# A two-layer transformer block on one core: first-layer gate as tanh straight from PSUM, second-layer low parts subtracted by GpSimd

## What is computed

```python
# layer 0, feed-forward: fp4_linear quantises both operands, then multiplies
gate = fp4_linear(x, w_gate)
y = fp4_linear(x, w_up)
h = jax.nn.silu(gate) * y
return fp4_linear(h, w_down)
# quantisation: scale = max(max|block| / 6, 1e-12); values go to the grid times scale

# layer 1, attention
q = (x @ Wq.T + bq).reshape(b, n, G, hpg, HD)
k = (x @ Wk.T + bk).reshape(b, n, G, HD)
scores = jnp.einsum('bqghd,bkgd->bghqk', q, k) * scale
attn = jax.nn.softmax(scores, axis=-1)
```

## Time and profile before

| | |
|---|---|
| runs | 1472.44 us median (1469.91 to 1474.29) |
| the profiled execution | 1470.66 us, its span 1468.9 us |
| TensorE busy | 1311.4 us (89%), 6337 matmuls |
| VectorE busy | 1088.7 us (74%), 2289 instructions |
| ScalarE busy | 845.8 us (58%), 1621 instructions |
| GpSimd busy | 110.8 us (8%), 227 instructions |
| chain that ended last | PE 71%, DVE 15%, ACT 7% |

### The profile page before, as it was taken

How to read it: one execution, slowest core, us unless ns; L and a number is a source line. 1 busy time by engine, 2 the same in 40 slices (tenths; PEclk the granted TensorE clock), 3 DMA queues, 4 the chain that set the end, 5 groups by cost and what they waited for, 6 DMA issues and landing times.

```text
span 1468.9 us, 19049 instructions
## 1 busy us (share of the span) xinstructions
PE 1311.4 (89%) x6337; PEld 563.3 (38%) x6337; DVE 1088.7 (74%) x2289; ACT 845.8 (58%) x1621; POOL 110.8 (8%) x227
## 2 busy tenths in 40 slices
PE   4688889889999965899999999999999999999884
PEld 3354445344443432433333333333433333333322
DVE  3677696688645668778888788888879888987324
ACT  2445535554555421177777666777666776777660
POOL 2010010001010100000000002000110000000033
PEclk9669899899999975689999999999999999999897
DMA  3000000000000000000000000000000000000000
GB/s 100 1 1 1 1 1 1 0 1 1 1 1 1 0 1 0 1 1 1 2 1 1 1 1 9 1 1 1 1 1 8 1 1 2 1 1 1 1 8 8
DMA packets 9010, 6.13 MB, mean 4 GB/s; under 512 B 2184, under 2 KB 8272, under 8 KB 8912
## 3 DMA queue, kind: packets, MB, share of 16 engines
q1 hardware_dynamic: 8912, 4.91, 1.2%
HBM read 3.66 MB, written 1.05 MB: 3 GB/s over the span
## 4 chain that ended last, share of the span: by engine, by line
PE 71%; DVE 15%; ACT 7%; issue 4%; POOL 1%; DMA 1%; SPq 1%; DVEq 0%; POOLq 0%; ACTq 0%
PE ps L749 24%; PE ps L730 16%; PE ps L650 8%; DVE MP L1161 7%; PE ps L726 6%; ACT PR L926 4%; PE ps L655 4%; PE ps L646 2%; PE ps L712 2%; ACT QO L825 1%; PE ps L661 1%; PE ps L679 1%; DVE ps L1158 1%; PE ps L615 1%; PE ps L690 1%
## 5 line engine op out<-in xcount | busy, mean ns | idle before, releaser
L926 ACT ACTIVATE PR<-ps 128x512 f32<-128x512 f32 (+2 forms) x1344 | 699.1, 585 | 414.1 <-PE ps L730 224.3
L1161 DVE TENSOR_REDUCE MP<-ps 128x1 f32<-128x512 f32 x1216 | 764.2, 682 | 133.9 <-PE ps L650 87.4
L749 PE MATMUL ps<-PR,V 128*32 128x512 f32 (+2 forms) x2688 | 435.6, 605 | 0.7 <-ACT OS L825 0.7
L730 PE MATMUL ps<-Q,KO 64*128 64x512 f32 x1024 | 363.1, 466 | 26.6 <-ACT PR L926 20.6
L650 PE MATMUL ps<-KO,Q 64*128 64x512 f32 x1024 | 354.5, 447 | 16.3 <-DVE MP L1161 12.2
L730 PEld LDWEIGHTS ps<-Q,KO 64*128 64x128 f32 x1024 | 153.6, 186 | 350.3 <-ACT PR L926 290.3
L650 PEld LDWEIGHTS ps<-KO,Q 64*128 64x128 f32 x1024 | 164.4, 191 | 85.0 <-DVE MP L1161 47.9
L726 PE MATMUL ps<-QO,KO 97*128 97x512 f32 (+3 forms) x320 | 144.7, 464 | 21.2 <-ACT PR L926 18.8
L655 PE MATMUL ps<-KO,QO 96*128 96x512 f32 (+2 forms) x320 | 127.9, 441 | 19.5 <-DVE QO L1137 13.7
L749 PEld LDWEIGHTS ps<-PR,V 128*32 128x32 f32 (+1 forms) x2688 | 74.1, 116 | 130.6 <-issue 60.4
L726 PEld LDWEIGHTS ps<-QO,KO 97*128 97x128 f32 x320 | 62.8, 201 | 152.0 <-ACT PR L926 97.0
(11 more groups left out here) (179 smaller groups left out, 748.7 us busy)
## 6 DMA issues: line engine op xcount, KB each, us to landing
Q<-MR SPq DMA_DIRECT2D x64, 2.0 KB
result<-V SPq DMA_DIRECT2D x4, 256.0 KB, 2.3
H<-in_L_attn_wq SPq DMA_DIRECT2D x1, 512.0 KB, 6.7
HQT<-in_L_attn_wo SPq DMA_DIRECT2D x1, 512.0 KB, 5.0
ew<-in_L_ffn_expert_w SPq DMA_DIRECT2D x1, 512.0 KB
bq<-in_L_attn_bq SPq DMA_DIRECT2D x12, 0.1 KB
wd<-in_L_ffn_w_down SPq DMA_DIRECT2D x1, 176.0 KB, 3.7
wg<-in_L_ffn_w_gate SPq DMA_DIRECT2D x1, 128.0 KB, 4.4
```

What stands on the lines that cost most here:

```text
L730: m = nc.tensor.matmul(dst[:, :], KO1[rows, g, kt * P:(kt + 1) * P], Q1[rows, it, h // 2, :], start=True, stop=True)
L749: nc.tensor.matmul(dst, VO[layer][:, kt, g, :], PR[:, u % NP_RING, q0:QC], start=kt == 0, stop=kt == key_tiles(layer, c) - 1).then_inc(pv_ ...
L926: nc.scalar.activation(PR[:, u % NP_RING, q0:QC], ps[:, 8 - nb + u % nb, q0:QC], ACT.Exp, scale=SCALE[layer]).then_inc(exp_done, 1)
L1161: v.tensor_reduce(MP[:, buf, h, q, kc:kc + 1], bank[:, 0:w], AX, ALU.max).then_inc(free, 1)
```

## The change

- **Gate.** ScalarE now writes `tanh(gate / 2)` from the PSUM bank to `H` for each of the four `gate` items. VectorE then computes `(H + 1) * bank`, which is twice SiLU, and frees the bank (L1185 of the new kernel). The step `silu` and its table loads are gone from the list. The factor two is taken out by a 0.5 where `down` is added to the residual (the instruction has three operands now, in `y0` with a factor of 1), and the quantiser's floor is 2e-12 for `H`.
- **Low parts.** For each `q1` and `k1` ScalarE first writes `bank + bias` as fp32 to one of two SBUF tiles (`WHOLE`), then the low part as before, and frees the bank. GpSimd waits for that and subtracts (L1047), and a new semaphore `tailed` tells PE (before its maxima) and ScalarE (before it reuses a tile, two items later). VectorE's `tails` are gone.
- **Buffers.** One of the two `WHOLE` tiles is the memory of the first-layer gate and up weights; the key-down and latent-up weights now load into memory of `H` and `HQT`.

```diff
-                    + gaps("2 3 1 1 1 1 2 1 1 1", [("xq", c)] + [("gate", q) for q in range(QT)] + [("silu",)]
+                    + gaps("2 3 1 1 1 2 1 1 1", [("xq", c)] + [("gate", q) for q in range(QT)]
                            + [("up", q) for q in range(QT)]))
...
+        WHOLE = (sb("WHOLE", [P, QC])[:, :], flat(wgu[:, 0:QC // D, :]))
...
-        IN_PARTS = ("q0", "k0", "k1", "q1")
+        IN_PARTS = ("q0", "k0")
+        BY_POOL = ("q1", "k1")
...
   (PE, before a max)
-                        if name in at:
+                        if name in tails_at:
+
+                            pe.wait_ge(tailed, tails_at[name])
...
   (ScalarE)
+                if kind == "gate":
+
+                    full()
+                    nc.scalar.activation(H[:, item[1], :], bank[:, 0:FF], ACT.Tanh, scale=0.5).then_inc(gated, 1)
...
+                if kind in BY_POOL:
+
+                    t = tails_at[0]
+                    if t >= len(WHOLE):
+                        act.wait_ge(tailed, t + 1 - len(WHOLE))
+                    dst, bias, low_bias, low = of_parts(item)
+                    nc.scalar.activation(WHOLE[t % len(WHOLE)], bank, ACT.Identity, bias=bias)
+                    i = nc.scalar.activation(dst, bank, ACT.Identity, bias=low_bias, scale=low)
+                    tails_at[0] += 1
...
-                    elif kind == "silu":
-
-                        j = gate_at[0]
-                        act.wait_ge(side_free[j % NS], n.side // NS + j // NS + 2)
-                        nc.scalar.activation(H[:, :, :], H[:, :, :], ACT.Silu).then_inc(act_out, 1)
...
   (GpSimd)
+                    if kind in BY_POOL:
+
+                        pool.wait_ge(side_free[k % NS], n.side // NS + k // NS + 2)
+                        dst = of_parts(step)[0]
+                        nc.gpsimd.tensor_tensor(dst, WHOLE[tails % len(WHOLE)], dst.bitcast(f32),
+                                                ALU.subtract).then_inc(tailed, 1)
+                        tails += 1
...
   (VectorE)
-            def tails(dst, bank, bias):
-
-                return v.scalar_tensor_tensor(dst, bank, bias, dst.bitcast(f32), ALU.add, ALU.subtract)
...
+                elif kind == "gate":
+                    h = H[:, item[1], :]
+                    dve.wait_ge(gated, n.gates + cnt.gates)
+                    v.scalar_tensor_tensor(h, h, 1.0, bank[:, 0:FF], ALU.add, ALU.mult).then_inc(free, 1)
...
                 elif kind in ("y0", "down"):
-                    link(v.tensor_tensor(R[:, :, :], tiles, chunk_of(item[1]), ALU.add))
+                    part = 1.0 if kind == "y0" else 0.5
+                    link(v.scalar_tensor_tensor(R[:, :, :], tiles, part, chunk_of(item[1]), ALU.mult, ALU.add))
```

More of the change, by code:

```diff
@@ L475, in __init__ @@
                 self.heads = sum(k in IN_PARTS for k in kinds)
+                self.tails = sum(k in BY_POOL for k in kinds)
                 self.rstd = sum(k in ("y0", "down", "y1", "stats") for k in kinds)
                 self.acts = sum(k in BY_SCALAR for k in kinds)
+                self.gates = kinds.count("gate")
                 self.logits = kinds.count("logits")
@@ L899, in side_item @@
                     i = copy(XQT[:, :], bank)
-                elif kind == "gate":
-                    i = copy(H[:, item[1], :], bank[:, 0:FF])
                 elif kind == "hqT":
@@ L1042, in link, with quantise @@
                 dve.wait_ge(chain, S["links"])
-            def quantise(stage, out, src, rows, width, end):
+            def quantise(stage, out, src, rows, width, end, least=1e-12):
                 nb = width // FB
```

67 lines of the change are left out of this document (34 added, 33 removed).

## The result

The changed kernel took 1477.14 us (median of 20 runs, 1471.33 to 1482.12) where the kernel before took 1473.35 (20 runs, 1469.52 to 1478.85). The ratio is 1.0029, with a 95% interval of 1.0015 to 1.0043: slower by some 4 us. Forecast were 1465.3 us, a range of 1451 to 1477, and a chance of 0.57 for faster. The mean of the four is 1.0019, so "0.1 to 0.3% slower" is what holds. Two executions in the whole record, of 1735 and 1893 us at a mean clock of 0.64 and 0.55, are left out of all ratios.

A forecast was written before the change was run, and what follows sets the result against it. PE was taken as the bound, with VectorE on the chain only beside layer 1's experts and ScalarE's exponentials throughout. Terms -7.0 + 3.2 - 5.0 + 1.5 + 0.1 = -7.2 gave 1463.5 us, or 1465.3 at the median; range 1451 to 1477.

The forecast's parts named there:

- Gate: Layer 0, chunks 0 to 3: removing SiLU and its table loads gains 7.0 us, range -2.1 to -14.
- 2.6 was forecast: Layer 0, chunk 2: gain from PE's 2.00 us idle at the SiLU and two slower passes behind it, 2.6 us.
- 1.3 was forecast: Layer 0, chunk 0: gain from PE's idle 0.97 and 0.32 us at the SiLU, taken as 1.3 us.
- first product with `up` 1.15 us behind the last tanh: Layer 0, chunk 3: tanh, wake-up and three-operand instruction take 1.15 us instead of 3.3, so 2.1 us gained.
- Keys: Low parts of 16 keys, layer 0 and its end: moving them to ScalarE and GpSimd costs 3.2 us, -2 to +6.
- 1.7 was forecast: Layer 0, chunk 2: last clip waits behind GpSimd's subtractions, so PE's last products come 1.7 us late.
- Queries: Layer 1, low parts of q1: VectorE's relief beside the experts gains 5.0 us, ScalarE's second activation costs 1.5.
- Rival A: Layer 1: each of 28 second activations costs its 0.60 us, 16.8 instead of 1.5; slower, 1480.5 us; chance 0.15.
- GpSimd's subtraction of 1.27 us delays nobody: Layer 1: some 27 maxima of other queries stand between a q1 and its first reader, so the subtraction costs nothing.
- Rival D: GpSimd's subtractions block VectorE instructions with two SBUF operands; five stops cost 6.4 us, 1471.7 us in all; chance 0.05.
- ScalarE's term: Layer 1: 0.60 us more per q1, 28 of 32 counted; five places at 0.3 give +1.5 us, range 0 to 17.
- rival C: Layer 0 gives nothing back: only chunk 3's 2.1 us remain, late clips cost twice 3.2; 1473.4 us; chance 0.16.

The follow-up runs named there:

- The mean of the four: Four timings of the changed kernel's instructions against the kernel before: 1.0029 and 1.0027 under its own name, 1.0014 and 1.0006 in two kernels with the same instructions.
- the empty step: Kernel before with the new gate, an empty step left in the list where the SiLU was: 1.0006 and 1.0004; the changed kernel with it: 1.0012.
- the one without their subtraction: New gate and moved buffers, VectorE's three-operand instruction of the 32 q1 left out and nothing in its place: 0.9929 of the kernel before.
- the kernel with the wait: Changed kernel, GpSimd's subtractions that follow an output chunk's normalisation in the list waiting until it is done: 0.9987 of the kernel before.
- another chain: New gate with moved buffers 0.9987; changed kernel with the queries' low parts back on VectorE 0.9978; changed kernel, mean of two timings, 1.0028.
- three pairs: Without and with GpSimd's wait for normalisations: keys back on VectorE 1.0008, 0.9987; changed kernel 1.0027, 0.9987; new gate plus unread subtractions 1.0020, 0.9951.
- the kernel with the extra subtraction: New gate with moved buffers, VectorE's tails kept, plus one unread GpSimd subtraction per q1: 1.0020 of the kernel before.

## Why the prediction was wrong

*Gate: forecast -7.0, measured -4.1* (0.9972, with -2 to -6.5 by single runs, and none with the empty step). The loads went, and PE's idle time behind the SiLU with them. The steps differ by chunk. Only chunk 2's can be read at a nearly level clock (0.98 before, 1.00 after): its stretch is 3.67 us shorter with the gate alone (71.10 against 74.77) and 2.52 in the changed kernel, which pays the 1.14 us for the two q1 there; 2.6 was forecast. Chunk 1's is 1.56 us shorter in the changed kernel's first profile and 1.4 longer in its second, so its 1.0 is neither borne out nor refuted. Chunk 0 gave nothing, where 1.3 was forecast: its stretch is 0.67 longer in the changed kernel and 0.6 to 2.3 in those of the gate alone. PE's idle time at the place shrank to 0.27 us, behind VectorE's product:

```profile
165.91 0.83 PE L695 MATMUL ps<-WUT,XQT 128*128 128x352 f32 x2 [0.27 <-DVE H L1188]
```

Why the stretch does not get shorter for it I have not settled. In chunk 3 the forecast had the first product with `up` 1.15 us behind the last tanh, as the earlier trace rows:

```profile
555.90 0.46 ACT L877 ACTIVATE H<-ps 128x352 f32<-128x352 f32 x1 [0.23 <-PE ps L695]
...
556.49 0.52 DVE L1185 SCALAR_TENSOR_TENSOR H<-H,ps 128x352 f32<-128x352 f32 x1 [0.17 <-ACT H L877]
557.05 0.69 DVE L1181 TENSOR_REDUCE MP<-ps 128x1 f32<-128x512 f32 x1
557.77 1.07 DVE L1188 TENSOR_TENSOR H<-H,ps 128x352 f32<-128x352 f32 x2
```

It is 1.87, for a maximum stands between them in VectorE's queue: 1.4 gained, not 2.1. What came of it hung on the clock: two profiles of the same gate-alone kernel have 154.01 us at 0.72 and 150.14 at 0.74 for the stretch that before took 152.61 at 0.73. A term of 2 us can't be read from one profile where PE switches between its two clock levels.

*Keys: forecast +3.2, measured -1.3 to +2.9 by the timings and +1.8 by the one stretch that can be read.* The step at the last clips of chunk 2 was right to a tenth: 1.7 was forecast. The other 1.5, for chunks 0, 1 and 3, lies where the clock moves, and no run shows it. ScalarE's last activation, GpSimd and PE, as the earlier trace rows:

```profile
520.26 0.77 ACT L888 ACTIVATE KO<-ps,bk_low,const 128x512 fp32r<-128x512 f32 x1
...
521.11 1.30 POOL L1047 TENSOR_TENSOR KO<-wgu,KO 128x512 fp32r<-128x512 f32 x1 [0.24 <-ACT KO L888]
522.37 0.29 POOL L1018 TENSOR_SCALAR_AFFINE_SELECT PR<-PR 128x128 f32<-128x128 f32 x1
...
522.71 0.43 PE L765 MATMUL ps<-PR,V 128*64 128x128 f32 x2 [0.58 <-POOL PR L1018]
```

1.81 us longer in every profile with the keys' subtraction on GpSimd, 0.0 in every one without.

*Queries: forecast -5.0 + 1.5, measured +3 to +7 by the timings.* The relief of VectorE was sized right (5.1 by the stretches). Rival A, at 16.8, is refuted by the plain iterations. At level clock the costs can be read too, in the kernel that moves the queries alone (keys back on VectorE) against the one without their subtraction: 1.0 us in each of the two iterations where a normalisation is stopped, 1.14 in layer 0's stretch with two q1, and 2.1 in five smaller pieces of 0.2 to 0.6 in layer 1's other iterations. That is 5.2 in all and eats the relief of 5.1. So the stretches that can be compared at one clock give 0, where the forecast had -3.5. The +3 to +7 of the timings are more than they explain. The rest would have to lie in how the clock falls, and that is open.

Two steps failed. The larger is the sentence "GpSimd's subtraction of 1.27 us delays nobody". It followed the result of the subtraction and asked who reads it. Nobody does for long. It did not ask what runs on VectorE meanwhile. Rival D had the mechanism in hand, a blocked port, at a chance of 0.05, and looked at the wrong place (the keys and the quantiser) and at the wrong instruction (two SBUF operands). What was stopped has one SBUF operand of size and two columns, and is a tensor_scalar. In the profile after, no subtraction ran beside a VectorE instruction with two SBUF operands, so rival D's own case was never met. The Trainium skill's page "SBUF — State Buffer" (section "Who interferes with whom") also names VectorE's two-port modes, which a tensor_scalar can enter, apart from two-operand instructions, as what keeps GpSimd and VectorE from running together. The trace agrees that such an instruction is stopped, with 1331 ns for 341; that it ran in such a mode no run here shows. I had read that page for its rule on two operands only: my sentence in rival D, that an instruction with at most one SBUF input does not contend, leaves out the page's exception for those modes. The normalisations into `X` and `R` never met a subtraction and took 345 and 341 ns on average.

The smaller step is ScalarE's term. It counted 28 of the 32 q1 and gave the four in layer 0 and at its end nothing, without a reason; two of them cost 1.14 us. Of the 2.1 us in small pieces, how much is ScalarE's second activation and how much a later expert sum is not parted.

Where the clock stayed at 1.00 behind a stop, the iteration took 56.98 us, 1.0 above the kernel with the wait, and where it was 0.97, 57.8 to 58.5. Kernels without a stop have this iteration at 0.97 as well, with 57.65 to 57.76 us, so the fall is not shown to come from the stop:

```profile
1085.03:1142.01 56.98, 54.85 (x279) 20.19 (x280) 47.84 (x86) 37.07 (x71) 12.29 (x15) 1.00 0.02 6
```

(This is the changed kernel's second profile.)

*Layer 0 as a whole.* The mark of rival C came true: layer 1's first score stands at 626.75 us in the profile after and at 625.75 before, where the forecast wanted it over 2 us earlier. C's mechanism fits chunk 0, where the idle time went and nothing was gained, but not chunk 2, with its 3.67 us. Against the gate stand the last clips' 1.81 us, the 1.14 of the two q1, and an opening that the forecast had at no cost. Up to the first output copy, three profiles with the changed kernel's instructions have 91.16, 90.86 and 91.24 us, against 89.33 before and 89.1 to 89.6 with the gate alone. The moved buffers by themselves don't do it (89.29 and 89.61), nor does it come with the wait or the empty step (88.59 and 89.53); why it is there is open.

*The sum.* -4.1 + 5.3 + 2.9 = +4.1 by one chain of kernels (gate alone 0.9972, with the queries moved 1.0008, with the keys too 1.0028). The forecast was -7.2. That the three add up is no evidence for any of them, since they are differences along one chain; another chain (0.9987, 0.9978, 1.0028) has -1.9, -1.3 and +7.4.

## What to carry to other kernels

Work that is moved to an idle engine has to be looked up twice: who waits for its result, and which SBUF-to-SBUF instructions of VectorE will run beside it; a wait that lets those go first was worth 1.0 us per meeting at level clock here, and 0.2, 0.4 and 0.7% in the timings of three pairs. Count every instance of an instruction that gets longer, not only those beside the stage that is looked at. Of the parts tried, the gate alone is the version to keep (0.9956, 0.9973 and 0.9987 in three timings), though its gain was not there with the empty step in the list (1.0006 and 1.0004). Where PE's clock moves between its levels, a difference of 2 us is a matter for many runs and for stretches at level clock, not for one profile.

## What the hardware showed unasked

- A VectorE tensor_scalar of 128x128 from SBUF took 1331 ns in place of 341 when it began 0.05 us behind the start of a GpSimd tensor_tensor of 128x512 from SBUF (1287 ns), and 341 when it had begun 0.2 us ahead of it. The layer-1 maxima, which read PSUM, never took over 693 in that profile.
- In the kernel with the extra subtraction, a VectorE tensor_reduce that reads SBUF (the quantiser's, at 445.6 us) ran beside one of them and took its usual 520 ns.
- 59 matmuls of the tail took 16.9 us at a clock of 0.73 or 21.4 at 0.62. Each of two kernels kept to its value in two profiles; their lists differ over 800 us earlier.
- A three-operand instruction with one operand in PSUM cost the same as the two-operand one: 521 ns over 352 columns for both, and 692 for the residual add.
- Over all timings, runs of one kernel differ by up to 14 us, and follow the mean granted clock: fits within kernels give 0.6 to 1.2 us for each 0.001, and 1.0 for all together.
